# Values as the stationary operand, probabilities normalised by accumulated row sums, and a longer-spread feed-forward chain in an AdaLN transformer block

## What is computed

```python
def local_attention(q, k, v):        # 16 heads of 64, windows of 32 tokens
    sim = einsum('bhwie,bhwje->bhwij', bq, bk2) * 8.0     # 32 queries x 64 keys
    sim = where(mask, -max, sim)
    attn = softmax(sim, -1)
    out = einsum('bhwij,bhwje->bhwie', attn, bv2)
for i in range(6):
    x = attn_layer(shift_tokens(x), ...) + x    # qkv = x @ Wqkv, l2norm, rotary, local attention, @ Wo
    x = ffn_layer(shift_tokens(x), ...) + x     # layernorm, x @ W1 + b1, a * gelu(gate) @ W2 + b2
```

## Time and profile before

| | |
|---|---|
| Time, three executions | median 2197.04 us (2187.98 to 2200.02) |
| The profiled execution | 2195.34 us, span 2193.1 us |
| PE busy | 2025.4 us, 92% of the span |
| DVE, ACT, POOL busy | 1545.8, 1407.1, 1225.7 us (70%, 64%, 56%) |
| DMA queue q1 | 16.2% of the 16 engines |
| Granted TensorE clock, mean | 0.973 |

### The profile page before, as it was taken

How to read it: one execution, slowest core, us unless ns; L and a number is a source line. 1 busy time by engine, 2 the same in 40 slices (tenths; PEclk the granted TensorE clock), 3 DMA queues, 4 the chain that set the end, 5 groups by cost and what they waited for, 6 DMA issues and landing times. The chain is left out here.

```text
span 2193.1 us, 84824 instructions
## 1 busy us (share of the span) xinstructions
PE 2025.4 (92%) x32996; PEld 1379.3 (63%) x32996; DVE 1545.8 (70%) x2879; ACT 1407.1 (64%) x4165; POOL 1225.7 (56%) x1376
## 2 busy tenths in 40 slices
PE   7788898999899999999998999998999989999986
PEld 3332335885775876766866758767668667587672
DVE  1598996885775866857857758668678577596673
ACT  5532235876675866756866758667678667586672
POOL 1465874764754754845646546548456465475450
PEclk9888789999999999999999999999999999999998
DMA  1311212111121211221111211112211111121110
GB/s 60 135 67 67 67 39 78 42 42 34 38 80 28 51 36 36 51 70 36 45 34 36 80 30 48 36 33 50 77 36 45 35 35 44 28 51 29 26 30 20
DMA packets 148100, 104.45 MB, mean 48 GB/s; under 512 B 15778, under 2 KB 140256, under 8 KB 146176
## 3 DMA queue, kind: packets, MB, share of 16 engines
q1 hardware_dynamic: 147712, 99.07, 16.2%
HBM read 48.31 MB, written 1.18 MB: 23 GB/s over the span
## 5 line engine op out<-in xcount | busy, mean ns | idle before, releaser
L1371 POOL TENSOR_TENSOR QK<-QK,RN 128x512 f32<-128x512 f32 x384 | 400.2, 1042 | 430.7 <-ACT RN L1112 413.9
L1122 ACT ACTIVATE PR<-ps,MN 128x64 f32<-128x64 f32 x1536 | 357.2, 316 | 166.0 <-DVE MN L1232 150.0
L1366 POOL TENSOR_TENSOR QK<-PC,PS 128x256 f32<-128x256 f32 x384 | 278.8, 726 | 304.7 <-PE ps L980 300.6
L994 PE MATMUL ps<-W,XS 128*128 128x256 f32 x1536 | 436.4, 407 | 5.2 <-PEq L64 4.1
L1148 ACT COPY QKT<-ps 128x512 f32<-128x512 f32 x384 | 224.8, 585 | 285.7 <-PE ps L980 285.4
L994 PEld LDWEIGHTS ps<-W,XS 128*128 128x128 f32 x1536 | 261.6, 190 | 62.5 <-issue 4.9
L1232 DVE TENSOR_REDUCE MN<-ps 128x4 f32<-128x256 f32 x384 | 162.6, 423 | 188.4 <-PE ps L948 186.3
L1256 DVE TENSOR_REDUCE SS<-SQ 128x8 f32<-128x512 f32 x384 | 260.9, 680 | 32.4 <-ACT SQ L1155 31.2
L1275 DVE TENSOR_TENSOR PC<-ps,TC 128x512 f32<-128x512 f32 x384 | 261.7, 682 | 28.2 <-POOL QK L1367 21.9
L1367 POOL TENSOR_TENSOR QK<-PC,PS 128x256 f32<-128x256 f32 x384 | 279.9, 729 | 0.0
L980 PE MATMUL ps<-ident,QK 128*128 128x128 f32 x1536 | 231.7, 273 | 38.0 <-POOL QK L1371 37.9
(11 more groups left out here) (137 smaller groups left out, 3221.0 us busy)
## 6 DMA issues: line engine op xcount, KB each, us to landing
V<-V SPq DMA_DIRECT2D x384, 97.5 KB, 2.2
scr<-B_rows SPq DMA_DIRECT2D x32, 512.0 KB, 3.6
V<-V SPq DMA_DIRECT2D x288, 32.5 KB, 2.0
W<-in_Wqkv SPq DMA_DIRECT2D x40, 192.0 KB, 2.8
TC<-in_tcos SPq DMA_DIRECT2D x6, 1024.0 KB, 5.1
TS<-in_tsin SPq DMA_DIRECT2D x6, 1024.0 KB, 7.5
WO<-in_Wo SPq DMA_DIRECT2D x6, 512.0 KB
W<-in_W SPq DMA_DIRECT2D x6, 341.0 KB, 3.6
```

The lines of the kernel that those rows point to most:

```text
L994: mm = nc.tensor.matmul(ps[:, par, k * 2 * P:(k + 1) * 2 * P], cols[k], W[:, i, 0:2, :].rearrange("p t m -> p (t m)"), start=True, stop=True)
L1122: e = nc.scalar.activation(PR[:, m % 2, h, slot * DH:(slot + 1) * DH], ps[:, 3 + h, slot * DH:(slot + 1) * DH], ACT.Exp, scale=-1.0, bias= ...
L1366: nc.gpsimd.tensor_tensor(QK[:, par, :, 0:hd], PC[:, par, :, 0:hd], PS[:, par, :, hd:DH], ALU.add)
L1371: nc.gpsimd.tensor_tensor(QK[:, par, :, :], QK[:, par, :, :], bcast_last(RN[:, m // 2 % 2, 8 * par:8 * par + 8], DH), ALU.mult).then_inc(q ...
```

## The change

Four things change in the transformer, all else stays.

1. `values` takes V (64 keys x 64 features) as the stationary operand and moves the 32 columns of PT. Its outputs then come with the features on partitions and the tokens as columns, as `out_proj` wants them. The tiles of the array are 64x64 in place of 64x32: four positions, where there were eight. `out_transposed`, the tile ON and the column of ones go; `copy_out` reads banks 5 and 6 directly, one iteration earlier (item n-7), and stands ahead of `exponents` in ACT's list.
2. The four activations of `exponents` also write the sum of their row (`accum_out`, RS). `normalise` works on the probabilities (item n-6): reciprocal of RS and product PR times RC in SBUF, between `least` and `clamp_pair` as before, and `p_transposed` of the same iteration waits for it (`prn`).
3. The chain after a phase is laid over more iterations: `out_proj` at u = 6 and 8, `mean` and `centre` at 7 and 9, `deviation` at 8 and 10, `var` at 10 and 12, `inverse` at 11 and 13, POOL's product at 12 and 14, its affine step at 13 and 15, the feed-forward at 16. The second `out_proj` waits for the first half's centring, not for its logarithm.
4. The feed-forward uses banks 2 and 7 in place of 7 and a projection bank; PE waits for the first half of its result ahead of the next `qk_transposed`, not for both halves ahead of the next `project`.

```diff
-U_WO, U_MEAN, U_VAR, U_FFN, U_TAB = (6, 9), (7, 11), (8, 12), 15, 20
+U_WO, U_MEAN, U_DEV, U_VAR, U_INV, U_Z, U_FFN, U_TAB = (6, 8), (7, 9), (8, 10), (10, 12), (11, 13), (12, 14), 16, 20
...
-        V = sb("V", [P, 16, 4, DH + 1])
+        V = sb("V", [P, 16, 4, DH])
...
-            def out_transposed(n):
-                m = n - 8
...
-                for k in range(2):
-                    src = ON[:, m % 2, :, :].rearrange("p (k h) d -> p k (h d)", k=2)[:, k, :]
-                    mm = nc.tensor.transpose(ps[:, 3, (1 + k) * P:(2 + k) * P], src, ident[:])
-                mm.then_inc(oT_ps, 1)
...
             def values(n):
...
-                wait(pe, on, m)
+                wait(pe, oT, m)
                 wait(pe, v_cp, min(n, NSTEPS))
-                for h in range(2):
-                    for slot, quad in spread_tiles:
+                for quad in range(4):
+                    for slot, h in ((0, 0), (1, 1), (0, 1), (1, 0)):
                         j = window(slot, quad)
                         r = slice(64 * slot, 64 * slot + 64)
-                        mm = nc.tensor.matmul(ps[32 * quad:32 * quad + 32, 5 + slot, h * (DH + 1):(h + 1) * (DH + 1)],
-                                              PT[r, m % 2, h, 32 * quad:32 * quad + 32],
-                                              V[r, 2 * (m % 8) + j // 4, 2 * (1 - j % 2) + h, :], start=True, stop=True)
+                        mm = nc.tensor.matmul(ps[DH * h:DH * h + DH, 5 + slot, quad * WIN:(quad + 1) * WIN],
+                                              V[r, 2 * (m % 8) + j // 4, 2 * (1 - j % 2) + h, :],
+                                              PT[r, m % 2, h, 32 * quad:32 * quad + 32], start=True, stop=True)
                 mm.then_inc(o_ps, 1)
...
             def project(n):
...
-                wait(pe, on, n - 6)
+                wait(pe, oT, n - 6)
...
             def p_transposed(n):
...
-                wait(pe, on, m)
-                pe.wait_ge(pr, m + 1)
+                wait(pe, oT, m)
+                pe.wait_ge(prn, m + 1)
...
             def out_proj(t, c):
...
                 if c == 0:
-                    wait(pe, x2, 2 * t - 1)
+                    wait(pe, x2, 2 * t)
                 if c == 1:
-                    pe.wait_ge(lnv, k0)
+                    pe.wait_ge(cen, k0)
...
             def var(t, c):
                 pe.wait_ge(fsq, k0 + 1)
-                pe.wait_ge(cen, k0 + 1)
+                if c == 0:
+                    pe.wait_ge(cen, k0 + 2)
+                if c == 1:
+                    pe.wait_ge(lnv, k0)
...
             def feed_forward(t, n):
-                banks = (7, (n + 1) % 2)
+                banks = (2, 7)
...
-                pe.wait_ge(prods, min(n, NSTEPS))
+                wait(pe, qkT, min(n - 3, NSTEPS))
...
             for n in range(NSTEPS + PHASE):
+                if u == U_FFN + 1 and t >= 0:
+                    pe.wait_ge(x2, 2 * t + 1)
                 qk_transposed(n)
-                out_transposed(n)
                 scores(n)
                 values(n)
-                if u == U_FFN + 1 and t >= 0:
-                    pe.wait_ge(x2, 2 * t + 2)
                 project(n)
                 p_transposed(n)
...
             def exponents(n):
...
                                                  ps[:, 3 + h, slot * DH:(slot + 1) * DH], ACT.Exp, scale=-1.0,
-                                                 bias=MN[:, m % 2, 2 * h + slot:2 * h + slot + 1])
+                                                 bias=MN[:, m % 2, 2 * h + slot:2 * h + slot + 1],
+                                                 accum_out=RS[:, m % 2, 2 * h + slot:2 * h + slot + 1])
...
             def copy_out(n):
-                m = n - 8
+                m = n - 7
...
-                act.wait_ge(oT_ps, m + 1)
-                act.wait_ge(s_ps, min(n - 4, NSTEPS))
-                act.wait_ge(mn, min(n - 4, NSTEPS))
+                act.wait_ge(o_ps, m + 1)
...
-                               ps[:, 3, P:3 * P].rearrange("p (k w c) -> p k w c", k=2, w=2)).then_inc(oT, 1)
+                               ps[:, 5:7, 0:P].rearrange("p s (w c) -> p s w c", w=2)).then_inc(oT, 1)
...
             for n in range(NSTEPS + PHASE):
                 norm_pair(n)
                 copy_qk(n)
+                copy_out(n)
                 exponents(n)
                 if u == U_FFN and t >= 0:
                     load_set(nc, act, GELU)
-                copy_out(n)
                 squares(n)
...
             def normalise(n):
-                m = n - 7
+                m = n - 6
...
-                dve.wait_ge(o_ps, m + 1)
-                o = ps[:, 5:7, 0:2 * (DH + 1)].rearrange("p s (h d) -> p s h d", h=2)
-                inv = RC[:, m % 2, :].rearrange("p (s h) -> p s h", s=2)
-                wait(dve, on, m - 1)
-                nc.vector.reciprocal(inv.unsqueeze(3), o[:, :, :, DH:DH + 1]).then_inc(rc, 1)
+                dve.wait_ge(pr, m + 1)
+                nc.vector.reciprocal(RC[:, m % 2, :], RS[:, m % 2, :]).then_inc(rc, 1)
                 dve.wait_ge(rc, m + 1)
-                wait(dve, oT_ps, m - 1)
-                nc.vector.tensor_tensor(ON[:, m % 2, :, :].rearrange("p (s h) d -> p s h d", s=2), o[:, :, :, 0:DH],
-                                        bcast_last(inv, DH), ALU.mult).then_inc(on, 1)
+                probs = PR[:, m % 2, :, :].rearrange("p h (s d) -> p (h s) d", s=2)
+                nc.vector.tensor_tensor(probs, probs, bcast_last(RC[:, m % 2, :], DH), ALU.mult).then_inc(prn, 1)
```

More of the change, by code:

```diff
@@ L795, in transformer_block @@
         PT = sb("PT", [P, 2, 2, P])
+        RS = sb("RS", [P, 2, 4])
         RC = sb("RC", [P, 2, 4])
-        ON = sb("ON", [P, 2, 4, DH])
         OUT = OT[:].rearrange("p c k m -> p (c k m)")[:, 0:T].rearrange("p (n m) -> p n m", m=D)
@@ L805, in transformer_block @@
         (qk_ps, v_ps, sq, v_cp, ss, ssm, lns, rn, prods, rot, qk, qkT_ps, qkT, s_ps, mn, pr, pT_ps, pT, o_ps,
-         rc, on, oT_ps, oT) = (sem("a_" + k) for k in (
+         rc, prn, oT) = (sem("a_" + k) for k in (
              "qk_ps", "v_ps", "sq", "v_cp", "ss", "ssm", "lns", "rn", "prods", "rot", "qk", "qkT_ps", "qkT", "s_ps",
-             "mn", "pr", "pT_ps", "pT", "o_ps", "rc", "on", "oT_ps", "oT"))
+             "mn", "pr", "pT_ps", "pT", "o_ps", "rc", "prn", "oT"))
         (q4, tabs, wo_ps, x1, mean_ps, cen, fsq, var_ps, lnv, rstd, z, xg, gate_ps, gel, up_ps, hid, w2_ps, x2) = (
@@ L814, in transformer_block @@
         stored = [sem("stored%d" % c) for c in range(NCH)]
-        s_vz, s_ones, s_v0, s_lnb = (
-            sem(k) for k in ("s_vz", "s_ones", "s_v0", "s_lnb"))
+        s_vz, s_pad, s_v0, s_lnb = (
+            sem(k) for k in ("s_vz", "s_pad", "s_v0", "s_lnb"))
         qkv_dram = d["Wqkv"].rearrange("l p (t i m) -> l p i t m", t=3, i=PAIRS)
@@ L862, in _ @@
             load_w2(0)
-            sp.wait_ge(s_ones, 2)
+            sp.wait_ge(s_pad, 1)
             sp.wait_ge(s_v0, 1)
@@ L938, in scores @@
                 if m == 0:
-                    pe.wait_ge(s_ones, 2)
+                    pe.wait_ge(s_pad, 1)
                 wait(pe, pr, m)
-                wait(pe, oT, m - 3)
                 for h in range(2):
@@ L1131, in copy_out @@
                 b, l, i, s, par = place(m)
-                act.wait_ge(oT_ps, m + 1)
-                act.wait_ge(s_ps, min(n - 4, NSTEPS))
-                act.wait_ge(mn, min(n - 4, NSTEPS))
+                act.wait_ge(o_ps, m + 1)
                 if i == 0 and m >= PHASE:
                     act.wait_ge(wo_ps, 2 * (m // PHASE - 1) + s // 2 + 1)
-                nc.scalar.copy(OT[:, s // 2, i, (s % 2) * STEP:(s % 2 + 1) * STEP].rearrange("p (w k c) -> p k w c", w=2, k=2),
-                               ps[:, 3, P:3 * P].rearrange("p (k w c) -> p k w c", k=2, w=2)).then_inc(oT, 1)
+                nc.scalar.copy(OT[:, s // 2, i, (s % 2) * STEP:(s % 2 + 1) * STEP].rearrange("p (w s c) -> p s w c", w=2, s=2),
+                               ps[:, 5:7, 0:P].rearrange("p s (w c) -> p s w c", w=2)).then_inc(oT, 1)
             def copy_qk(n):
@@ L1170, in copy_v @@
                 if n < 6:
-                    act.wait_ge(s_ones, 2)
+                    act.wait_ge(s_pad, 1)
                 wait(act, o_ps, n - 7)
@@ L1215, in _ @@
                     for c in range(2):
-                        if u == U_MEAN[c] + 1:
+                        if u == U_DEV[c]:
                             deviation(t, c)
-                        if u == U_VAR[c]:
+                        if u == U_INV[c]:
                             inverse(t, c)
@@ L1339, in _ @@
             nc.gpsimd.memset(VEC[:], 0.0).then_inc(s_vz, 1)
-            nc.gpsimd.memset(V[:, :, :, DH:DH + 1], 1.0).then_inc(s_ones, 1)
-            nc.gpsimd.memset(QKT[:, :, 0:PAD], 0.0).then_inc(s_ones, 1)
-            pool.wait_ge(s_ones, 2)
+            nc.gpsimd.memset(QKT[:, :, 0:PAD], 0.0).then_inc(s_pad, 1)
+            pool.wait_ge(s_pad, 1)
```

(8 more changed lines are left out.)

## The result

The changed kernel takes 2214.15 us (median, 2208.86 to 2215.05) against 2196.57 of the kernel before: a ratio of 1.0081, 95% interval 1.0048 to 1.0114. That is slower by 0.8%, where the forecast was 2190, slightly faster. It lies in the range given and in the forecast case's own range, 24 us from the point and on the wrong side of no change.

A forecast was written before the change was run, and what follows sets the result against it. PE bounds plain steps before; ACT's chain was to become the bound at 3.46 us. Plain steps +27, phases -30 and tail -2 gave a 2188 us span, 2190 with 2.2 around it, against 2197.04; range 2105 to 2300.

The forecast's parts named there:

- the forecast case's own range: Whole kernel: ACT's chain as the bound at 3.38 to 3.55 us a plain step, 2150 to 2240 us, chance 0.50.
- The layout on PE: PE in a plain step: output transposes off 0.21, values on four positions +0.17, step 3.26 us from 3.30.
- the drain between tilings: PE's values: changing from 64x32 to 64x64 tiles drains the engine; stands with the slower-values rival, +0.33 us or more, chance 0.09.
- The sums and the loop on ACT: Row sums cost 0.09 us per exponent; copy_out waits for values; plain steps 3.42 even, 3.49 odd, mean 3.46 us.
- The gaps ahead of the values that end with V's copy: Sign in plain steps: PE idles before the values until ACT's V copy ends.
- DVE: DVE's two instructions stay alike in size (ON 0.42 us), P transposes now wait for them, cost nothing.
- the 0.67 of cover: Plain step: DVE's product ends 1.55 us after the scores' start, P transposes start at 2.22.
- the rivals: Sums cost a whole instruction, 2320 to 2360 us (0.16); sums nearly free, 2103 to 2140 (0.25); values slower, 2237 to 2310 (0.09).
- The chain: Steps u = 6 to 17 of each phase: 77.2 us against 79.9, -2.7 a phase, -30 over 11 phases.
- The tail: After the last steps: second projection starts about 3.5 us earlier, but variance and logarithm then follow it, -2 us.
- The sum: Whole span: plain steps +27, phases -30, tail -2, so 2193.1 - 5 = 2188 us.

## Why the prediction was wrong

*The layout on PE* was right: 3.25 a step against 3.26, with 0.19 more for entering and doing the values against 0.17. No more than that can be said of the drain between tilings that was weighed there: the 0.19 holds it and the longer loads together.

*The sums and the loop on ACT* were right in mechanism and size: 0.09 for each, `copy_out` waiting for the values, 3.46 for a plain step. Odd and even steps both take 3.46, not 3.49 and 3.42. The gaps ahead of the values that end with V's copy, a sign that the prediction named, are there too.

*DVE* is the step that failed: "Its two instructions stay alike in size (ON 0.42) but now P transposes of the same iteration wait for them", and the 0.67 of cover, "Cost nothing". The product did not stay alike. With both inputs in SBUF it lasts up to 1.29, median 0.80, and eats the cover where `add_attn` or the feed-forward's additions already had DVE late: 0.5 at u = 7, 9 and 17 in each of 11 phases, 17 us. With the rest of its effect the product costs 26 to 30, by two runs. The three steps are 0.7 longer each, not only the 0.5 of the wait, which makes 22 to 23, and 5.5 come from POOL: its first addition is stretched in turn, and the 20 steps in which POOL rescales tables are POOL's to set.

A sign of it stood in the kernel before. This row, by source line, is DVE's clamp, 16 columns wide, in and out of SBUF:

```profile
L1263 DVE TENSOR_SCALAR SS<-SS x192: 164/598/759, 366.7 to 2119.1; 128x16 f32<-128x16 f32 x192
```

while the product that read PSUM took 424 every time. An instruction of constant size whose duration varies fourfold is waiting inside for something. The 45 of the 192 clamps that no POOL instruction overlaps take 164 to 167 ns. The Trainium skill (SBUF — State Buffer, Who interferes with whom) states the rule: VectorE's second SBUF read port is the one that GpSimd uses, and a VectorE instruction with two SBUF inputs and a GpSimd instruction that reads SBUF exclude each other. The runs agree, in both directions (0.42 to 0.80 median, 0.73 to 0.85 mean). The clamp has one such input and so is not that sentence's case; it showed that the two engines disturb each other, not how much the product would suffer. The rule speaks against this change and should have stood among the rivals.

*The chain* by itself is worth more than I gave it, not less: 3.5 a phase alone, 43 us in all, where I had 2.7 as part of the whole. In the changed kernel without the product it is still 79.93 - 76.78 = 3.1. So the difference of 1.2 against 2.7 in the changed kernel is the product's doing, not the chain's. *The tail* was given -2: from the last step's QK transposes to the end it takes 70.3 against 68.0, +2.3. The new order gives little: in the run with the longer chain alone the tail takes 67.6, at a granted clock of 0.88 (0.89 before), since the variance and logarithm that I put behind the second projection are followed by the second half's own, one after the other. The rest is not the chain's. In the changed kernel the last steps take 1.8 longer up to the first projection, and the granted clock of the tail is 0.81.

The sum, then: -5 was forecast for the span, +13.7 was found. By stretches of the two profiled runs: the eleven with the chain -21.2 in place of -30, and 8 of these 21.2 are three stalls of PE at u = 6 in the profile before (12.4 us and more for the step, in place of 10.2), which the forecast did not count; the eleven of twenty steps +29.4 in place of 24, the excess from the table steps; the other steps +4.7 in place of 3; the tail +2.3; the Mamba block -1.5. A small slip besides: the 1.7 by which the profiled execution lies below the median was not added back, the forecast's own sum is 2192.

Without the product the changed kernel takes 2186.6, 3 us from the point forecast. That is in part luck, since the stalls, the chain's better worth and the tail had been left out or put wrong and nearly cancel.

*The whole ladder* in medians: 2196.6 before; 2152.7 with the chain; 2117.5 with the transposed layout as well and no normalisation; 2186.6 with the sums; 2214.2 with the product. What sums and product cost depends on the order in which they are added, by 10 us.

Left open: how much of the values' 0.19 is the change of tiling, which no run separated; and what the stalls at u = 6 are, of which the profile of the changed kernel has next to none.

## What to carry to other kernels

A change that moves an elementwise step from PSUM to SBUF can put it in the way of another engine: look in the trace for durations that vary at constant size on VectorE and GpSimd, and count how many inputs of each instruction lie in SBUF. And when an engine that is second by 5% gets new work, ask whether its idle time stands where the work comes: the same row sums cost some 25 us where the idle time could take them and 59 where a new wait had used it up. Last, when a change has parts, price and try each alone; here the parts that pay hid behind two that cost.

## What the runs showed of the hardware

Reading out a row sum occupies 212 ns in the record but adds only 0.09 us to the distance of two exponents (0.20 to 0.30). DVE's and POOL's stretching is mutual: a product of 256 columns with both inputs in SBUF takes 424 to 1291 ns beside POOL, 424 to 426 with one of them in PSUM, and POOL's first addition has a mean of 850 and 727. 32 records of 32 moving columns on four 64x64 positions take 0.60 to the next group, 32 of 65 columns on eight 64x32 positions 0.46: with fewer positions and twice the columns to load, half the moved columns did not make it shorter, and 0.06 more passes from the scores to them.
